# Opening with lengths taken without the rms and context pieces moved to the prologue; first cross attention with four copies in flight, far keys in 32 pieces and leading pairs copied

## The chip, the core and the metric

The kernel is one program on one core of a Trainium2 chip. The metric is device time in microseconds, lower is better. A core has TensorE (PE), VectorE (DVE), ScalarE (ACT), GpSimd (POOL) and SyncE (SP), which here issues nearly all transfers, and 16 DMA engines. The engines run their own instruction lists in order and wait for one another by semaphores that the kernel sets by hand.

## The reference

A decoder of two layers on `x` of 1024 tokens x 128 features, with 6404 context rows of 96 features. Each layer adds an attention-like block, a cross attention and a mixture of experts, each behind a layer norm. The change touches the first two blocks of layer 0:

```python
# block 1: fast weights (4 heads of 32, chunks of 256 tokens)
qkv = hidden @ qkv_w.T; q, k, v = split(qkv)
q, k = rms_norm(q, q_norm_w), rms_norm(k, k_norm_w)   # x * rsqrt(mean(x*x) + eps) * w, over 128 features
q, k = l2_normalize(heads(q)), l2_normalize(heads(k)) # x / (norm(x) + 1e-5), over 32 features
lr = softplus(hidden @ lr_proj_w.T + lr_proj_b + c)   # three rates per head and token
for each chunk:                                       # output with the weights W0, W1, W2 so far, then
    dw0, dw1, dw2 = gradients of the chunk with the rates; five Newton-Schulz rounds each
    W = (W + dw) renormalised to its first row lengths
# block 2: cross attention, 8 heads of 16, 1024 queries, 6404 keys
q, k, v = ln(x) @ Wq + bq, ctx @ Wk + bk, ctx @ Wv + bv
x = x + softmax(q k^T / 4) v @ Wo + bo
```

The second cross attention (layer 1) uses the same context with other weights (`wkv1`, 8 heads of 64, normalised keys).

## The kernel before

The program is a row of stages, each a block of five instruction lists: `opening_stage`, `xattn0_stage`, `moe0_stage` and three more. A stage starts on all engines when the one before has ended on all. The diff touches the first two.

**Opening.** It does two jobs at once. Job one is block 1: layer norm, the projections, rms norm, lengths and rates (the prologue), three updates of the fast weights (chunks 0 to 2), the outputs of the last chunk, and the queries of the first cross attention, which are split into three bf16 parts, stored to `q0_dram` and read back as `qs` and `qm` (the tail). Job two, the context, projects 52 tiles of 128 context rows to keys and values of both cross attentions and stores them in DRAM. `context()` on each engine is a generator; `Filler` takes pieces of it at named points of job one: `fill("ms")` takes as many pieces as the table `FILLS` says for "ms". Each engine uses the same table. A tick is four pieces, and there are 55 ticks for 52 tiles, since a tile passes through several ticks; so there are 220 pieces. The tables before give 37 pieces to the prologue (`FILLS`), 50 to each update and 26 to the tail (`FILLS_END`); the 7 left are run by `fill.rest()`. In a tick, PE computes `a_V` (L562, L563: keys and values of this stage's cross attention), `a_K` (L570) and `a_V` again (L574) and transposes (L581); ACT evacuates; DVE sums squares and scales; POOL splits the keys in four operations (L357 to L360) and raises sums to the power -1/2 (L365).

In the prologue DVE multiplies `qkv` with the rms factor (L814), then with the norm weight (L817); ACT squares it, DVE sums the squares to lengths (L833), ACT takes roots (L484), DVE divides (L840). POOL computes the rms factor (L374). `rated` (L846) multiplies keys or values with a rate, one instruction for each of 8 tiles, for three outputs.

The first context matmul waits for nine loads (`load_c`), the last being `null_v`. SP issues one broadcast of the byte mask `real` of 6656 columns to 96 partitions before the first context tiles.

In the tail SP waits for the first half of the split queries, stores it to `q0_dram` (L306), later reads it back and so lets the next stage begin.

**First cross attention.** The softmax needs a maximum for each query and head. Keys lie in SBUF as `ks` (and `ks0` for the first 2048 columns of the near heads, loaded in the opening). The near heads are 0 to 3 and the far heads 4 to 7. There are four units (head group x half of the queries); a unit has 104 pairs, each pair being two matmuls (L1192) of 128 queries by 496 keys for two heads, whose maxima are wanted, and 52 tiles of scores (L1210), exponentials (L1164) and weighting (L1223).

Unit 0's pairs come before any score. Of each four, three are matmuls into `psE`, copied as bf16 to `copied` by ACT (L1153) and merged into `running` by DVE (L1320); the fourth goes to one of three banks `psM` and is reduced by DVE (L1305). With `copied` of two slots, ACT waits for the merge of two pairs earlier:

```python
if n >= 2:
    e.wait_ge(pre_merged, n - 1)
```

Then DVE folds `running` (L1327, L1330), gives the maxima (L1338 to L1346), PE transposes them, ACT copies them to `mrow` (L1135), and SP writes them into rows of `qs` (L1107); the first scores wait for that (`m_placed`). Between, twelve pairs of unit 1 (`LEAD`) are computed and reduced. In each tile of units 0 to 2 two or three pairs of a later unit are computed and reduced between the scores (`in_tile`), so that the pairs of unit 2, the first that needs far keys, begin near tile 44 of unit 0.

SP issues near key block 1, the queries of units 1 to 3, near blocks 2 and 3, and all far keys in eight transfers of 832 KB; then, in each unit, the three rows of maxima and the value tiles, two tiles at a time, each when the tiles two turns back are used.

## Time and profile before

| | |
|---|---|
| median of 3 runs | 2792.28 us (2788.86 to 2794.58) |
| profiled execution, its own time | 2790.04 us |
| its span | 2788.3 us |
| PE busy | 2408.3 us (86%) |
| DVE busy | 2085.6 us (75%) |
| ACT busy | 1536.6 us (55%) |
| POOL busy | 297.7 us (11%) |

Times in the trace are microseconds from the span's start. The opening runs to 365.4 us, the first cross attention from there to about 1010 us, the other stages fill the rest. Busy time is the union of an engine's instructions in a stretch; the number in brackets behind it counts instructions. The PE clock is the granted share of full speed. In a timeline row the first number is the start, the second the length, in brackets stands the idle time of the engine just before and what ended it. SPq is the queue of SP's transfers.

### The profile page before, as it was taken

The numbers are of one execution on the slowest core, as the hardware profiler recorded it, in microseconds if no ns is written. First come the engines' busy times: TensorE is split into PE (matmuls) and PEld (weight loads), VectorE is DVE, ScalarE is ACT, GpSimd is POOL, SyncE is SP. The second block draws the span as 40 slices with busy tenths as digits, with TensorE's granted clock in tenths as the row PEclk, the third lists the DMA queues.
The fourth block names the chain that finished last, engine by engine and source line by source line (L and its number), as shares of the span: only waits on it lengthen the run. The fifth ranks groups of instructions, "written<-read, shape, count | busy, mean of one in ns | idle before, by whom it ended". The sixth has DMA issues, their size and how long they took to land. (4 is left out here: it accounts for less than half of the span.)

```text
span 2788.3 us, 34759 instructions
## 1 busy us (share of the span) xinstructions
PE 2408.3 (86%) x10287; PEld 892.3 (32%) x10344; DVE 2085.6 (75%) x3063; ACT 1536.6 (55%) x1850; POOL 297.7 (11%) x330
## 2 busy tenths in 40 slices
PE   5888755999999979999566579999999999997998
PEld 3555411222222224444223123333333333332443
DVE  5666678999997023344597789999999999977675
ACT  5544565776767953333343466666676766654111
POOL 4655600000000000000055000000000000000000
PEclk8988955999999989999688679999999999998998
DMA  4344498000000107766100522013113111111100
GB/s 116 129 137 136 136 154 93 25 25 25 25 23 27 31 26 190 192 192 181 25 0 5 124 65 58 27 42 92 29 30 89 43 29 29 29 35 36 80 1 8
DMA packets 186929, 190.79 MB, mean 68 GB/s; under 512 B 18496, under 2 KB 158981, under 8 KB 185473
## 3 DMA queue, kind: packets, MB, share of 16 engines
q1 hardware_dynamic: 186653, 188.97, 26.2%
q8 instruction: 78, 1.28, 0.2%
q14 instruction: 54, 0.44, 0.1%
q10 hardware_dynamic: 144, 0.10, 0.0%
HBM read 144.12 MB, written 41.42 MB: 67 GB/s over the span
## 5 line engine op out<-in xcount | busy, mean ns | idle before, releaser
L2520 DVE TENSOR_TENSOR y_acc<-y_acc,y_probs 128x1024 f32<-128x1024 f32 x408 | 496.5, 1217 | 34.0 <-ACT y_probs L2216 23.7
L2216 ACT ACTIVATE y_probs<-y_E,y_mask_bias 128x1024 f32<-128x1024 f32 x416 | 441.2, 1112 | 66.3 <-PE y_E L2301 47.1
L1164 ACT ACTIVATE x_probs<-x_E 128x1024 f32<-128x1024 f32 x408 | 396.8, 1021 | 137.0 <-PE x_E L1210 134.3
L1305 DVE TENSOR_REDUCE x_maxima<-x_M 128x1 f32<-128x496 f32 x676 | 420.5, 668 | 25.4 <-PE x_M L1192 14.0
L2310 PE MATMUL y_O<-y_probs,y_values 128*64 128x512 f32 x1664 | 402.3, 604 | 0.0
L2300 PE MATMUL y_E<-y_qa,y_ks 128*128 128x512 f16 x832 | 319.5, 384 | 1.2 <-ACT y_copied L2192 1.2
L2301 PE MATMUL y_E<-y_qb,y_ks 66*128 66x512 f16 x832 | 317.7, 382 | 0.0
L2192 ACT ACTIVATE y_copied<-y_M 128x1024 bf16<-128x1024 f32 x164 | 167.9, 1024 | 209.7 <-PE y_M L2267 209.7
L2458 DVE TENSOR_REDUCE y_maxima<-y_M 128x2 f32<-128x1024 f32 (+1 forms) x195 | 238.8, 1224 | 35.6 <-PE y_M L2267 23.4
L1629 DVE TENSOR_TENSOR f_hidden<-f_act_out,f_spread 128x512 f32<-128x512 f32 x160 | 110.7, 692 | 169.5 <-ACT f_act_out L1513 161.9
L1223 PE MATMUL x_O<-x_probs,x_values 128*32 128x512 f32 x1632 | 217.3, 605 | 0.9 <-ACT x_probs L1164 0.6
L1513 ACT ACTIVATE f_act_out<-f_b 128x512 f32<-128x512 f32 x160 | 95.4, 597 | 185.1 <-PE f_b L1545 185.1
L1210 PE MATMUL x_E<-qs,x_keys 128*128 128x512 bf16 x641 | 177.6, 382 | 8.9 <-issue 3.8
L2267 PE MATMUL y_M<-y_ks,y_qa 64*128 64x512 f16 x742 | 148.6, 397 | 26.4 <-DVE y_maxima L2458 23.7
L1550 PE MATMUL f_b<-f_hidden,f_weights 128*128 128x512 f32 x320 | 164.1, 596 | 5.0 <-DVE f_hidden L1629 5.0
L1545 PE MATMUL f_b<-f_xnT,f_weights 128*128 128x512 f32 x320 | 165.2, 598 | 1.1 <-ACT f_act_out L1513 1.1
L2310 PEld LDWEIGHTS y_O<-y_probs,y_values 128*64 128x64 f32 x1664 | 101.5, 136 | 171.2 <-issue 159.7
L2469 DVE TENSOR_TENSOR y_running<-y_running,y_copied 128x1024 bf16<-128x1024 bf16 x192 | 131.3, 684 | 3.7 <-ACT y_copied L2192 3.4
L1192 PE MATMUL x_M<-x_keys,qs 64*128 64x496 bf16 x298 | 117.0, 393 | 12.7 <-DVE x_maxima L1305 12.6
L2300 PEld LDWEIGHTS y_E<-y_qa,y_ks 128*128 128x128 f16 x832 | 81.6, 98 | 141.5 <-issue 45.5
L2713 PE MATMUL g_b<-g_w_in,g_xnT 128*128 128x512 f32 x256 | 117.7, 605 | 5.1 <-DVE g_gate L2783 3.9
L2267 PEld LDWEIGHTS y_M<-y_ks,y_qa 64*128 64x128 f16 x742 | 35.8, 93 | 259.7 <-DVE y_maxima L2458 174.4
(471 smaller groups left out, 3179.4 us busy)
## 6 DMA issues: line engine op xcount, KB each, us to landing
f_spread<-comb_dram SPq DMA_DIRECT2D x160, 256.0 KB, 3.9
y_values<-v_dram SPq DMA_DIRECT2D x208, 128.0 KB, 2.2
v_dram<-a_v_out SPq DMA_DIRECT2D x26, 512.0 KB, 2.7
k_dram<-a_k_parts SPq DMA_DIRECT2D x26, 512.0 KB, 3.4
x_values<-v_dram SPq DMA_DIRECT2D x100, 128.0 KB, 2.1
f_weights<-f_w_in SPq DMA_DIRECT2D x80, 128.0 KB, 2.3
y_ks<-k_dram SPq DMA_DIRECT2D x75, 128.0 KB, 2.9
v_dram<-a_v_out SPq DMA_DIRECT2D x26, 256.0 KB, 2.0
```

The lines of the kernel that those rows point to most:

```text
L1164: nc.scalar.activation(probs[:, n % 2, 2 * g:2 * g + 2, :], psE[:, 2 * g:2 * g + 2, :], ACT.Exp).then_inc(exped, 1)
L1210: ins = T.matmul(psE[:, j, :], key_tile(4 * (u // 2) + j, t), qs[:, u, j, :], start=True, stop=True)
L1223: ins = T.matmul(psO[32 * j:32 * j + 32, :], values[:, i, 32 * j:32 * j + 32], probs[:, n % 2, j, :], start=(t == 0), stop=(t == TILES0 - ...
L1305: V.tensor_reduce(maxima[:, 2 * h + j, qt, c:c + 1], psM[(2 * entry + j) % 3][:, 0:CHUNK0], AX.X, ALU.max).then_inc(max_done, 1)
L2192: A(out, scores, ACT.Copy).then_inc(S["spare_copied"], 1)
L2216: A(probs[:, i, :], psE[:, 2 * (i % 2):2 * (i % 2) + 2, :].rearrange("p a b -> p (a b)"), ACT.Exp, bias=mask_bias[:, bass.ds(c * TILES_IN_ ...
L2267: ins = T.matmul(out[:, j, :], qa[r, u, j, q0:q0 + P], ks1[r, u // 2 % 2, c * 512 + KVP * j:c * 512 + KVP * j + 512], start=True, stop=True)
L2300: T.matmul(psE[:, 2 * slot + j, :], ks1[:, u // 2 % 2, keys], qa[:, u, j, :], start=True, stop=False)
L2301: ins = T.matmul(psE[:, 2 * slot + j, :], ks2[:, u // 2 % 2, keys], qb[:, u, j, :], start=False, stop=True)
L2310: ins = T.matmul(psO[u % 2][DH1 * j:DH1 * j + DH1, :], values[:, i, DH1 * j:DH1 * j + DH1], probs[:, i, 512 * j:512 * j + 512], start=Fals ...
L2458: V.tensor_reduce(maxima[:, u % 2, :, 2 * g, bass.ds(c, 1)], psO_pair[:] if (u, g) == (0, 1) else psM[:], AX.X, ALU.max)\
L2520: ins = V.tensor_tensor(acc[:, u % 2, :], acc[:, u % 2, :], probs[:, i, :], ALU.add)
```

## The change

Opening: the tables move 17 context pieces from the tail and the rest to the prologue. The product with the norm weight comes first and alone; lengths are taken of it, and the rms factor enters through the 64 lengths (times rms, plus 1e-5, reciprocal, times rms). The `rated` products become one instruction each. The roots of the first weights are taken with those of the lengths, and small ACTIVATE instructions on `table` place table loads. `real` is broadcast in two parts, and `null_v` moves to the later list of loads.

First cross attention: `copied` gets four slots; eight of the twelve leading pairs are copied by ACT to `lead_max` and folded by DVE in four parts in unit 0's tiles 2, 4, 6 and 8; near blocks 2 and 3 are issued ahead of the queries; far keys are loaded in 4 blocks of 8 pieces, one behind each of the value loads 2 to 33.

```diff
-FILLS = (("stats", 4), ("xn", 2), ("proj0", 4), ("proj1", 4), ("sums", 4), ("ms", 4), ("qk", 4), ("hs", 3),
-         ("tr0", 4), ("tr1", 4))
+FILLS = (("stats", 4), ("xn", 3), ("proj0", 4), ("proj1", 4), ("sums", 6), ("ms", 8), ("qk", 6), ("hs", 6),
+         ("tr0", 6), ("tr1", 7))
-FILLS_END = (("last0", 4), ("last1", 4), ("q_stats", 4), ("q_norm", 4), ("q_tr", 5), ("q_split", 5))
+FILLS_END = (("last0", 2), ("last1", 2), ("q_stats", 3), ("q_norm", 3), ("q_tr", 3), ("q_split", 3))
-        LOADS_C, LOADS = 9, 10
+        LOADS_C, LOADS = 8, 11
-                sp.dma_start(real[0:CTX, :], d.real_keys.partition_broadcast(CTX)).then_inc(spread_real, 16)
+                sp.dma_start(real[0:CTX, INVERT_AT[0]], d.real_keys[INVERT_AT[0]].partition_broadcast(CTX))\
+                    .then_inc(spread_real, 16)
...
+                sp.dma_start(real[0:CTX, REST], d.real_keys[REST].partition_broadcast(CTX)).then_inc(spread_rest, 16)
-                e.wait_ge(to_sqrt, 1)
-                ACTIVATE(ninit[:], wn[:], ACT.Sqrt).then_inc(from_sqrt, 1)
...
+                e.wait_ge(s_qk, 1)
+                e.wait_ge(to_pow, 2)
+                ACTIVATE(sq[:], qk[:], ACT.Square).then_inc(s_sq, 1)
                 fill("ms")
...
-                e.wait_ge(s_qk, 1)
-                ACTIVATE(sq[:], qk[:], ACT.Square).then_inc(s_sq, 1)
                 fill("qk")
                 e.wait_ge(to_sqrt, 2)
-                ACTIVATE(hn[:], hs[:], ACT.Sqrt).then_inc(from_sqrt, 1)
+                ACTIVATE(ninit[:], wn[:], ACT.Sqrt)
+                ACTIVATE(hn[:], hs[:], ACT.Sqrt).then_inc(from_sqrt, 2)
+                ACTIVATE(table[:], half[:, 0:1], ACT.Sigmoid)
...
+                        if r == 2:
+                            ACTIVATE(table[:], half[:, 0:1], ACT.Sqrt)
...
                     ACTIVATE(wr[:], wn[:], ACT.Sqrt).then_inc(from_sqrt, 1)
+                    ACTIVATE(table[:], half[:, 0:1], ACT.Sigmoid)
...
+                V.tensor_tensor(qk[:].rearrange("p t a b -> p t (a b)"), qkv[:, :, 0:256],
+                                norm_w[:].unsqueeze(1).to_broadcast([P, TILES, 256]), ALU.mult).then_inc(s_qk, 1)
...
-                fill("ms")
-                e.wait_ge(from_pow, 2)
-                step(V.tensor_tensor(qk[:], qkv[:, :, 0:256].rearrange("p t (a b) -> p t a b", a=2),
-                                     rms[:].rearrange("p (t a) -> p t a", a=2).unsqueeze(3)
-                                     .to_broadcast([P, TILES, 2, P]), ALU.mult))
...
+                step(V.tensor_tensor(heads(hn), heads(hn), by_rms, ALU.mult))
                 step(V.tensor_scalar(hn[:], hn[:], 1e-5, None, ALU.add))
                 step(V.reciprocal(hs[:], hn[:]))
+                step(V.tensor_tensor(heads(hs), heads(hs), by_rms, ALU.mult))
+                fill("hs")
...
-        copied = sb("copied", [P, 2, 2, CHUNK0], BF16)
+        copied = sb("copied", [P, 4, 2, CHUNK0], BF16)
+        lead_max = sb("lead_max", [P, 8, 2, CHUNK0], BF16)
...
-                load_keys(near, KEY_BLOCKS[1], keys_in[1])
+                for b in (1, 2, 3):
+                    load_keys(near, KEY_BLOCKS[b], keys_in[b])
...
-                load_keys(far, slice(0, KVP), far_keys_in)
...
+                        if 2 <= g < 2 + 4 * (len(K_ROWS) + 1):
+                            load_far_piece(g - 2)
...
-                    if n >= 2:
-                        e.wait_ge(pre_merged, n - 1)
-                    nc.scalar.activation(copied[:, n % 2, :, :], psE[:, 2 * (n % 2):2 * (n % 2) + 2, 0:CHUNK0],
+                    if n >= 4:
+                        e.wait_ge(pre_merged, n - 3)
+                    nc.scalar.activation(copied[:, n % 4, :, :], psE[:, 2 * (n % 2):2 * (n % 2) + 2, 0:CHUNK0],
...
+                for i in range(COPIED_LEAD):
+                    n = 3 * EARLY + i
+                    e.wait_ge(pre_mm, 2 * n + 2)
+                    nc.scalar.activation(lead_max[:, i, :, :], psE[:, 2 * (n % 2):2 * (n % 2) + 2, 0:CHUNK0],
+                                         ACT.Copy).then_inc(pre_copied, 1)
...
+                def fold_lead(part):
+                    width = CHUNK0 >> part
+                    if part == 0:
+                        e.wait_ge(pre_copied, 3 * EARLY + COPIED_LEAD)
+                    if part < 3:
+                        step(V.tensor_tensor(lead_max[:, :, :, 0:width // 2], lead_max[:, :, :, 0:width // 2],
+                                             lead_max[:, :, :, width // 2:width], ALU.max))
+                    else:
+                        for h in range(2):
+                            ins = V.tensor_reduce(maxima[:, 2 * h:2 * h + 2, 0:4, 0].rearrange("p j q -> p q j"),
+                                                  lead_max[:, 4 * h:4 * h + 4, :, 0:width], AX.X, ALU.max)
+                        step(ins)
```

## Rows read from the trace of the kernel before

**Rows 1.** Busy time of each engine in stretches: instructions in brackets, PE clock, DMA share, GB/s.

```profile
78.70:157.90 79.20, 67.20 (x321) 44.60 (x320) 53.27 (x104) 40.92 (x95) 49.18 (x67) 0.94 0.43 138
...
365.40:458.80 93.40, 55.26 (x210) 10.91 (x210) 76.89 (x131) 72.66 (x78) 0.27 (x1) 0.50 1.03 130
...
481.00:893.00 412.00, 392.58 (x2365) 100.09 (x2412) 385.73 (x633) 293.75 (x306) 2.54 (x2) 1.00 0.09 24
```

**Rows 2.** Timeline of one turn of the maxima loop: start, length, engine, line, count.

```profile
442.73 0.68 DVE L1320 TENSOR_TENSOR x_probs<-x_probs,x_copied 128x992 bf16<-128x992 bf16 x1 [0.54 <-ACT x_copied L1153]
...
443.32 1.25 DVE L1305 TENSOR_REDUCE x_maxima<-x_M 128x1 f32<-128x496 f32 x2
...
444.48 1.25 DVE L1320 TENSOR_TENSOR x_probs<-x_probs,x_copied 128x992 bf16<-128x992 bf16 x2
...
445.24 2.80 ACT L1153 ACTIVATE x_copied<-x_E 128x992 bf16<-128x992 f32 x3 [0.75 <-PE x_E L1192]
446.27 0.68 DVE L1320 TENSOR_TENSOR x_probs<-x_probs,x_copied 128x992 bf16<-128x992 bf16 x1 [0.54 <-ACT x_copied L1153]
```

**Rows 3.** Timeline from the loop's end to the first scores of unit 0.

```profile
458.79 3.26 DVE L1327 TENSOR_TENSOR x_probs<-x_probs 128x2976 bf16<-128x2976 bf16 x3
...
464.57 0.19 DVE L1346 CAST x_mpf<-x_mpart 128x48 f32<-128x48 bf16 x1
...
466.03 0.27 ACT L1135 ACTIVATE x_mrow<-x_M 48x128 bf16<-48x128 f32 x1 [9.15 <-PE x_M L1230]
...
467.07 13.50 DVE L1305 TENSOR_REDUCE x_maxima<-x_M 128x1 f32<-128x496 f32 x20 [1.02 <-PE x_M L1192]
...
480.98 1.48 PE L1210 MATMUL x_E<-qs,ks 128*128 128x512 bf16 x3 [0.34 <-issue]
```

**Rows 4.** Single lines: lengths in ns (least, median, most), first and last start.

```profile
L1327 DVE TENSOR_TENSOR x_probs<-x_probs x3: 547/935/1708, 458.8 to 461.5; 128x2976 bf16<-128x2976 bf16 x1, 128x1488 bf16<-128x1488 bf16 x1, 128x744 bf16<-128x744 bf16 x1
...
L1330 DVE TENSOR_REDUCE x_maxima<-x_probs x2: 532/538/543, 462.1 to 462.5; 128x6 f32<-128x372 bf16 x2
...
L846 DVE TENSOR_TENSOR a_xn<-a_qk,a_lrate x8: 282/284/291, 66.9 to 68.3; 128x128 f32<-128x128 f32 x8
```

**Rows 5.** DMA issues in 367 to 371.4: KB each, median us to landing.

```profile
x_keys<-key_ones_in SPq DMA_DIRECT2D x1, 248.0 KB, 15.1
```

**Rows 6.** DMA issues in 100 to 250, the opening.

```profile
ks<-k_dram SPq DMA_DIRECT2D x7, 256.0 KB, 5.0
```

**Rows 7.** DMA issues in 480 to 1000, the units.

```profile
qs<-x_mrow SPq DMA_DIRECT2D x9, 4.0 KB, 1.8
```

**Rows 8.** Timeline of the prologue: the first context matmul and the rms products.

```profile
12.40 2.07 PE L570 MATMUL a_K<-a_wkv,a_ctx_real 97*128 97x512 f32 x2 [12.40 <-DMA a_null_v<-null_v_in]
...
45.55 2.29 DVE L814 TENSOR_TENSOR a_qk<-a_qkv,a_rms 128x2048 f32<-128x2048 f32 x1 [0.53 <-POOL a_rms L374]
45.59 2.53 POOL L357 TENSOR_TENSOR a_kr<-a_kf,a_k_parts 128x128 f32<-128x128 f32 x1
...
51.70 0.37 ACT L439 ACTIVATE a_kf<-a_V,a_bk 128x128 f32<-128x128 f32 x1 [7.60 <-POOL a_k_parts L360]
```

**Rows 9.** Timeline of the opening's tail: the queries' own chain.

```profile
323.39 0.41 DVE L867 TENSOR_TENSOR x<-x,a_b 128x256 f32<-128x256 f32 x1
...
327.20 1.64 DVE L56 BATCH_NORM_STATS2 a_stats<-x 128x6 f32<-128x128 f32 x8
...
329.87 1.65 POOL L374 TENSOR_TENSOR a_rstd<-a_var,a_mhalf 128x8 f32<-128x8 f32 x1 [1.22 <-DVE a_var L61]
...
333.87 2.80 DVE L67 TENSOR_SCALAR a_xn<-x,a_moments,a_rstd 128x128 f32<-128x128 f32 x8
...
338.74 0.60 ACT L537 ACTIVATE a_xnT<-a_b 128x512 f32<-128x512 f32 x1 [0.26 <-PE a_b L725]
...
342.53 1.88 PE L730 MATMUL a_b<-a_xnT,a_wq 128*128 128x512 f32 x4
...
355.69 0.68 SPq L306 DMA_DIRECT2D q_dram<-a_q_parts  x1
```

More of the change, by code:

```diff
@@ L1096, in _, with load_far_piece @@
                     sp.dma_start(dst, src).then_inc(load, 16)
-                for b in (2, 3):
-                    load_keys(near, KEY_BLOCKS[b], keys_in[b])
-                load_keys(far, slice(0, KVP), far_keys_in)
+                def load_far_piece(n):
+                    b, piece = n // (len(K_ROWS) + 1), n % (len(K_ROWS) + 1)
+                    cols, loaded = FAR_BLOCKS[b], far_keys_in[b]
+                    if piece < len(K_ROWS):
+                        load_key_rows(sp, d, ks[:, far, cols], far, cols, *K_ROWS[piece], loaded)
+                    else:
+                        load_key_ones(sp, d, ks[:, far, cols], cols, loaded)
                 for u in range(UNITS):
@@ L1375, in _ @@
                         merge(3 * (p // 4) + p % 4, p)
-                take(1, 0, EARLY)
-                pass_on(m_row, 1, EARLY + 1)
-                for p in range(1, LEAD):
-                    take(1, p, EARLY + 1 + p)
+                pass_on(m_row, 1, EARLY)
+                for p in range(COPIED_LEAD, LEAD):
+                    take(1, p, EARLY + 1 + p - COPIED_LEAD)
                 for u in range(UNITS):
```

72 lines of the change are left out of this document (40 added, 32 removed).

## Prediction

> **What bounds the kernel now.** I read the table by stage first, then the timelines of the stretches that the diff touches, then single lines and the transfers. The reader should see four stretches. The opening stage (0 to 365.4 us) keeps no engine full: in an update of 79.2 us PE is busy 67, DVE 53, POOL 49 [rows 1]. Its length is that of a chain of dependent small steps into which pieces of the second job, the keys and values ("context"), are threaded on every engine in a fixed order. The maxima before the first softmax tile (365.4 to 458.8) are a loop of 26 turns of four pairs. One turn is 3.54 us, from DVE's 442.73 to its 446.27; in it ACT makes three copies in 2.80 us and then stands, and DVE does five operations 0.59 us apart (2.93 us) and then waits 0.54 us for ACT [rows 2]. Each waits for the other, because the two copy buffers let ACT run only two pairs ahead, and DVE spends 1.17 us of each turn on the fourth pair, which it reduces straight from PSUM. Third comes the hand-over, 458.8 to 481: DVE folds alone, then reduces twelve leading pairs of the next unit at 1.36 us each, with PE waiting, before the first scores at 480.98 [rows 3]. Last come the units: in 481 to 893 DVE is busy 386 of 412 us and PE 393, so DVE work added there is paid [rows 1].
>
> **The loop with four copies in flight.** ACT may now be four pairs ahead. It needs three copies, 2.80 us less the overlap, near 2.7 us a turn; DVE needs 5 x 0.585 = 2.93 us. PE issues the fourth pair only when DVE has freed a bank, about half a microsecond before DVE's turn ends, which still leaves ACT its 2.7 us. I take 2.95 us a turn: 26 x (3.54 - 2.95) = 15.3 us saved. Bounds: 2.93 gives 15.9; if the order on PE (three copied pairs, then the one that waits for DVE) holds ACT up by half of its present wait, the turn is 3.3 and 6 us are saved; a loss is excluded, since no wait is added.
>
> The cover is the arrival of keys. The last piece of key block 1 is issued at 370.9 and lands 15.1 us later, at 386.0 [rows 5]; PE's first matmul of turn 8 needs it. PE runs one turn ahead of DVE, whose first operation is at 367.3: 367.3 + 7 x 2.95 = 388.0. Blocks 2 and 3 are now issued right behind it instead of behind 27 query transfers. Two MB took 16 us there, so block 2 (2 MB) is in near 402, wanted at 413; block 3 (0.7 MB) near 408, wanted at 436; the queries (1.5 MB) near 420, wanted at 441. Nothing is late, with 2 us to spare at the tightest place; a late block would cost its lateness once.
>
> **The leading pairs.** Eight of twelve go through ACT into a buffer of their own, 8 x 0.9 = 7.2 us, while DVE does its 6.0 us of folding and splitting of unit 0's maxima (458.79 to 464.76) [rows 3]. ACT starts some 2 us before DVE ends the loop, so it is free within the time in which DVE gives the maxima. The transpose of the maxima no longer waits for a leading pair's reduction, which saves 0.7 us. After the row of maxima is copied (466.03 + 0.27) the scores now start 14.7 us later [rows 3]. With four pairs left: 0.1 + 3 x 1.36 + 0.6, and the gap of 0.3 that stands before the scores now, 5.2 us. The row's own transfers must have landed too: three issues 1.9 us and 1.8 us to land when the queue is quiet [rows 7], 3.7 us, below 5.2. (Before, they landed behind the 6.8 MB of far keys.) Saved: 14.7 - 5.2 + 0.7 = 10.2 us. If the transfers still meet queries it is 8.
>
> **What it costs: the fold.** DVE halves 16 x 496 values three times and reduces the rest in unit 0's tiles 2, 4, 6 and 8. The halvings of the present fold took 1.708, 0.935 and 0.547 us for 2976, 1488 and 744 values [rows 4], that is 0.16 + 0.52 us a thousand. For 3968, 1984 and 992: 2.22 + 1.19 + 0.68 = 4.1 us; two reductions of 496 values by the 0.538 us for 372: 1.3 us. Sum 5.4 us. Of it DVE's idle share of unit time, 6% [rows 1], hides a little: 5 us on the path. Bounds 3 and 5.4 us. The banks just turn by two; the sequence of pairs is unchanged.
>
> **Far keys in 32 pieces.** They leave the start, where the DMA engines are full (share 1.03 [rows 1]), and follow value loads 2 to 33, one every two tiles (5.2 us). A piece is 213 KB. A piece of 256 KB of the same kind took 5.0 us to land in the opening [rows 6], so one of 213 is in before the next value load is issued. The value load goes out ahead of its piece. The first far chunk is wanted near tile 44 of unit 0, its eight pieces are issued by tile 18; the fourth block is issued by tile 14 of unit 1 and wanted near tile 32. I cost this at nothing; the cover is the 5.2 us of two tiles.
>
> First cross attention: -15.3 - 10.2 + 5.0 = -20.5 us (-22 to -10).
>
> **The opening.** The context job has 220 pieces (55 ticks of four). Before: 37 in the prologue, 150 in three updates, 26 in the tail and 7 left over. After: 54, 150, 16, 0. So 17 pieces move ahead of the updates, and since the last ticks only finish tiles, the tail keeps little but its own chain.
>
> Tail. Its delays can be read [rows 9]: the statistics start at 327.20 though the sum was done at 323.80 (3.4 us); the norm is applied at 333.87 though its power was done at 331.52 (2.3); the query matmul starts at 342.53 though its input was done at 339.34 (3.2). From there, first half out of PE (1.0), two copies (1.3) and four splitting steps (2.5) would allow the store to q_dram at 347.5; it is issued at 355.69 (8.2). Sum 17.1 us of context ahead of the chain. Sixteen pieces remain with about two ticks of real work, which cost some 2 us: -15 us. Bounds: -17 (all) and -11 (a third stays). The 9.7 us from that store to the next stage's start stay.
>
> Prologue. Seventeen pieces cost at least POOL's work per piece in an update, 49.2 / 50 = 0.98 us, and at most an update's pace, 79.2 / 50 = 1.58 us [rows 1]: 17 to 27 us. Against that: the first context matmul waits until 12.40 for null_v, the last of nine loads, behind a 639 KB broadcast [rows 8]; null_v leaves the list and the broadcast shrinks to 160 KB, about 2.4 us. The product of 2048 values with the rms (2.29 us) goes, replaced by two of 64 values; and lengths no longer wait for POOL's power. In the present trace that product and the next hold POOL's 0.43 us subtraction for 2.53 us and ACT waits 7.60 us for POOL [rows 8]: some 5 of these 7.6 go. The 24 rate products of 0.28 us [rows 4] become three of about 1.15 us (half of 2.29): 1.5 us, as part lies beside the transposes. The savings sum to 11 to 13 us. Net +4 to +16; I take +9, since ticks in the prologue ran slower than POOL's floor. What is late next is POOL, whose 54 pieces need 53 us at least in the 78 behind the first.
>
> The table switches only move: one Sqrt in the prologue falls away (1.28 us of ACT), the others stand where ACT had slack. I cost them at nothing (0 to 1.3 us gained).
>
> On the port: in [rows 8] POOL's subtraction took 2.53 us, and ended with DVE's 2048-value product. The Trainium skill (SBUF — State Buffer, section SBUF: two separate sides) says that a DVE operation with two SBUF inputs and a GpSimd one exclude each other for a whole instruction. That speaks against merging eight short products into one. By that rule POOL can be held up to 1.15 us three times, where it slipped between the short ones before; the sum would be 2 to 3 us worse in the prologue.
>
> Opening: +9 - 15 = -6 us (-14 to +4).
>
> **Sum.** -20.5 - 6 = -26.5 us against the profiled execution's own 2790.0: 2763.5. That execution lies 2.2 us under the median of the three runs, 2792.3, whose counterpart is 2765.8. Everything behind the first cross attention keeps its code; I expect 2765.
>
> **Rivals.**
> 1. The prologue takes the moved pieces at an update's pace with few savings (+15) and the tail keeps a third of its delay (-11): the opening gives +4, total -16.5, 2776. For it: the prologue's nine ticks take 66 us now, 12.4 to 78.7. Against: 7.6 us of one of them are the wait that goes. Chance 0.17.
> 2. The loop stays bound by the round of PE, ACT and bank release (3.3 us a turn): 10 us less, 2775. For it: PE's fourth pair waits for DVE, in order, in front of the next copied one. Against: five DVE operations fill 2.93 us, and only the copies were late. Chance 0.15.
> 3. The opening hides nearly all moved pieces (+2, -16): 8 us more, 2757. For it: DVE and ACT have a third idle. Chance 0.13.
> 4. Slower: far pieces hold up value loads. If a piece and the value load behind it took longer than the 5.2 us of two tiles, each excess would be paid 32 times; the gain of 26.5 us is gone from 0.83 us each. At 7 us per pair of transfers: 32 x 1.8 = 58 us, 2823. For it: 5.0 us to land for 256 KB. Against: most of these 5.0 us shared the DMA engines with the opening's stores, and loads overlap. Chance 0.04.
> 5. No change: fold, late keys and a full prologue together eat the gain, as if the four buffers bought nothing. Chance 0.02.
>
> **How the numbers follow.** The forecast as worked has 0.49; its own range is 2757 to 2771. The 8-in-10 range takes in rivals 1 and 2 up to 2779 and rival 3 down to 2751. A change under 0.2% (5.6 us) can't be told from none by such runs. Faster 0.94, same 0.02, slower 0.04.
>
> **What would show it.** A loop turn of 2.95 us with ACT never waiting for DVE; first scores some 90 us after the loop's first matmul instead of 115.4; four DVE operations on lead_max in tiles 2 to 8 with PE waiting there; no DMA share of 1.0 beyond the first 55 us of the stage; the first update's start near 88 instead of 78.7; from the last update's end (now 315.4) to the q_dram store 25 us instead of 40.3. Wrong would be: ACT waits that stay, value loads with a landing above 4 us, or a prologue beyond 95 us.

## The result, and the profile after

The changed kernel took 2743.65 us (median of 4 runs, 2743.25 to 2745.59), the kernel before 2791.59 (4 runs, 2788.86 to 2794.58): a ratio of 0.9829 with a 95% interval of 0.9812 to 0.9846. It is 48 us faster. The prediction, 2765 with a range from 2751 to 2779, is wrong: the direction holds, but the gain lies beyond the range. The profiled execution took 2743.25 us, its span is 2741.5.

Cutting both spans (2788.3 and 2741.5) at the same instructions shows where the 46.8 us come from. The updates are measured from the first Sigmoid of the first update to the last copy into `w1t_bd` of the third.

| stretch | before | after | change | forecast |
|---|---|---|---|---|
| start to the first update | 79.98 | 88.38 | +8.4 | +9 |
| three updates | 235.4 | 219.6 | -15.8 | 0 |
| tail, to the first matmul of the next stage | 50.2 | 33.2 | -16.9 | -15 |
| loop of the maxima | 93.2 | 77.8 | -15.4 | -15.3 |
| hand-over to the first scores | 22.2 | 11.85 | -10.35 | -10.2 |
| units, first scores to the first of the two sum matmuls that end them | 530.8 | 538.1 | +7.4 | +5 |
| everything behind | 1776.6 | 1772.5 | -4.1 | 0 |

Four of the five terms of the sum came out within 2 us; the updates were never in the sum. Their three lengths, cut at the starts of the same instructions and added up, show in which steps the time went. `gsum` is the sum of the squared gradient, `X` its normalised form, `wsq` the squared new weights, the root that of their row sums. e3, e5 and e12 are runs told below.

| step of the three updates, us | before | after | e3 | e5 | e12 |
|---|---|---|---|---|---|
| to `gsum` | 54.3 | 46.6 | 56.8 | 47.8 | 45.1 |
| `gsum` to `X` | 12.8 | 12.3 | 12.7 | 12.3 | 12.3 |
| `X` to `wsq`, with five rounds | 132.7 | 130.3 | 138.2 | 133.0 | 131.8 |
| `wsq` to the root | 13.9 | 9.9 | 11.9 | 13.2 | 13.2 |
| root to its use on DVE | 4.8 | 2.6 | 9.3 | 1.2 | 1.2 |
| use to the last copies | 16.9 | 17.9 | 16.9 | 18.8 | 19.0 |

Windows of the kernel after, with the columns of [rows 1]: the first update, the loop of the maxima, and the first 412 us of the units.

```profile
88.40:163.00 74.60, 63.91 (x313) 42.48 (x312) 52.48 (x103) 39.00 (x94) 47.65 (x67) 0.95 0.51 161
341.40:419.00 77.60, 58.14 (x216) 11.00 (x212) 74.71 (x130) 74.13 (x81) 0.00 (x0) 0.50 0.69 87
430.90:842.90 412.00, 388.54 (x2322) 98.74 (x2364) 384.80 (x625) 287.41 (x299) 2.52 (x2) 0.99 0.15 40
```

In the loop DVE is busy 74.7 of 77.6 us and ACT 74.1, where in [rows 1] they stood 16.5 and 21 us; the DMA share is 0.69 instead of 1.03. In the units DVE and PE are as busy as before, so what is added there is paid. The first update does the same work per engine within 4 us, and from its Sigmoid to that of the second are 74.6 us where there were 77.4 (79.98 to 157.37).

Timeline of one turn of the loop, which answers to [rows 2].

```profile
410.77 5.69 ACT L1171 ACTIVATE x_copied<-x_E 128x992 bf16<-128x992 f32 x6
...
411.89 1.25 DVE L1331 TENSOR_REDUCE x_maxima<-x_M 128x1 f32<-128x496 f32 x2
...
413.06 1.83 DVE L1346 TENSOR_TENSOR x_probs<-x_probs,x_copied 128x992 bf16<-128x992 bf16 x3
...
414.81 1.25 DVE L1331 TENSOR_REDUCE x_maxima<-x_M 128x1 f32<-128x496 f32 x2
```

From 411.89 to 414.81 is a turn of 2.92 us (forecast 2.95). No DVE row has a wait any more, and the six copies of ACT touch each other. The 0.54 us of waiting on ACT's copy is gone from DVE.

Timeline from the loop's end to the first scores, which answers to [rows 3].

```profile
416.60 7.22 ACT L1176 ACTIVATE x_lead_max<-x_E 128x992 bf16<-128x992 f32 x8
...
419.01 3.26 DVE L1353 TENSOR_TENSOR x_probs<-x_probs 128x2976 bf16<-128x2976 bf16 x3
...
425.48 0.27 ACT L1153 ACTIVATE x_mrow<-x_M 48x128 bf16<-48x128 f32 x1 [1.65 <-PE x_M L1253]
...
426.48 5.34 DVE L1331 TENSOR_REDUCE x_maxima<-x_M 128x1 f32<-128x496 f32 x8 [1.50 <-PE x_M L1215]
...
430.86 1.49 PE L1233 MATMUL x_E<-qs,ks 128*128 128x512 bf16 x3 [0.33 <-issue]
```

ACT copies the eight leading pairs (7.22 us) beside DVE's folding, as the sum had it. From the row of maxima (425.75) to the scores are 5.1 us, forecast 5.2.

Single lines of the fold, and the transfers of 480 to 970, which answer to [rows 4] and [rows 7].

```profile
L1365 DVE TENSOR_TENSOR x_lead_max<-x_lead_max x3: 666/1184/2215, 443.4 to 458.3; 128x3968 bf16<-128x3968 bf16 x1, 128x1984 bf16<-128x1984 bf16 x1, 128x992 bf16<-128x992 bf16 x1
L1369 DVE TENSOR_REDUCE x_maxima<-x_lead_max x2: 660/660/660, 463.9 to 464.5; 128x8 f32<-128x496 bf16 x2
```

```profile
x_values<-v_dram SPq DMA_DIRECT2D x91, 128.0 KB, 2.2
x_keys<-k_dram SPq DMA_DIRECT2D x21, 208.0 KB, 3.7
```

The halvings take 2.22, 1.18 and 0.67 us (forecast 2.22, 1.19, 0.68) and the two reductions 1.32 (forecast 1.3). A far piece lands in 3.7 us, inside the 5.2 of two tiles, and a value load in 2.2.

Timeline of the opening: the first context matmul, and the tail that answers to [rows 9].

```profile
9.34 2.05 PE L576 MATMUL a_K<-a_wkv,a_ctx_real 97*128 97x512 f32 x2 [9.34 <-DVE a_ctx_real L754]
```

```profile
313.29 0.42 DVE L873 TENSOR_TENSOR x<-x,a_b 128x256 f32<-128x256 f32 x1 [0.60 <-PE a_b L645]
...
314.95 1.63 DVE L56 BATCH_NORM_STATS2 a_stats<-x 128x6 f32<-128x128 f32 x8
...
330.78 0.54 SPq L308 DMA_DIRECT2D q_dram<-a_q_parts  x1
```

The statistics start 1.2 us after the sum instead of 3.4, and the store to `q_dram` comes 22.8 us after the last update instead of 40.3.

So the question is why three updates whose own code is nearly the same take 15.8 us less. Two things could have changed them: the pieces of context work beside each step, and the three small activations on `table`.

### The profile page after: what moved, and what is told of

The parts are those of the page before. It is cut to its first block and busy times, and to the rows that moved or that the text cites. A ratio compares the mean times of both kernels' runs of the same rounds, so it can differ in the third digit from the quotient of the medians.

```text
span 2741.5 us, 34784 instructions
## 1 busy us (share of the span) xinstructions
PE 2398.3 (87%) x10287; PEld 882.6 (32%) x10344; DVE 2072.4 (76%) x3032; ACT 1539.8 (56%) x1863; POOL 295.2 (11%) x330
## 3 DMA queue, kind: packets, MB, share of 16 engines
q8 instruction: 78, 1.28, 0.2%
## 5 line engine op out<-in xcount | busy, mean ns | idle before, releaser
L1331 DVE TENSOR_REDUCE x_maxima<-x_M 128x1 f32<-128x496 f32 x660 | 409.8, 667 | 28.0 <-PE x_M L1215 17.4
```

What stands on the lines that cost most here:

```text
L1331: V.tensor_reduce(maxima[:, 2 * h + j, qt, c:c + 1], psM[(2 * entry + j) % 3][:, 0:CHUNK0], AX.X, ALU.max).then_inc(max_done, 1)
```

## The experiments

Two names are used below. The *position* of an update is the number of a tick's four pieces that are already taken when it starts: 37 pieces ahead leave 1, and since an update takes 50, the next stands at 3, the third at 1. With 54 pieces ahead the positions are 2, 0, 2. *Tables* are the activations on `table`. Lengths of single updates run from the end of the one before (for the first, from its Sigmoid).

### The two stages apart, and the tables alone

The theory at this point was that order or amount of the moved pieces shortens the updates; the rival, that the table loads do.

**e1_opening_only** and **e2_xattn_only** take one stage from each kernel:

```diff
 # e1: the opening of after, and from here on the code of before
-        copied = sb("copied", [P, 4, 2, CHUNK0], BF16)
+        copied = sb("copied", [P, 2, 2, CHUNK0], BF16)
...
 # e2: the opening of before, and from here on the code of after
-FILLS = (("stats", 4), ("xn", 3), ("proj0", 4), ("proj1", 4), ("sums", 6), ("ms", 8), ("qk", 6), ("hs", 6),
-         ("tr0", 6), ("tr1", 7))
+FILLS = (("stats", 4), ("xn", 2), ("proj0", 4), ("proj1", 4), ("sums", 4), ("ms", 4), ("qk", 4), ("hs", 3),
+         ("tr0", 4), ("tr1", 4))
...
```

> The changed opening with the first cross attention of before. The trace of the changed kernel puts 24.3 us of the gain in the opening (first matmul of the next stage at 341.2 us instead of 365.6). If the two halves of the change are independent, this kernel gains 24 us and its next stage starts at 341.2 us; the loop of maxima keeps its 3.54 us a turn. If the far keys and the opening interact (shared DMA engines, the state of the PE clock), the sum of this kernel's and the other half's gains differs from the whole by more than 3 us.

> The opening of before with the changed first cross attention. By the changed kernel's trace its loop takes 2.92 us a turn and the stretch from the stage's first matmul to the first scores shrinks by 25.8 us, the units pay 7.4 us: net 18 us gained, stage to the end of unit 3 from 646.2 us to 627.8. If the halves are independent it is 18 us within 2 us; if the earlier start of the stage matters it is less.

e1 took 2763.51 us (ratio 0.991, 0.9894 to 0.9927), e2 2769.06 (0.9928, 0.9911 to 0.9945), the kernel before on that chip 2788.58. The gains are 25.1 and 19.5 us; their sum, 44.6, is 3 us short of the whole, which is what such medians scatter. The opening of e1 ends at 340.78, that of after at 341.22: the updates owe nothing to the next stage. In e2 the units took 535.9 us, 2.2 less than in the profile of after with the same code; that comes back below.

**e3_tables_only** is the kernel before with the small activations:

```diff
                 ACTIVATE(hn[:], hs[:], ACT.Sqrt).then_inc(from_sqrt, 1)
+                ACTIVATE(table[:], half[:, 0:1], ACT.Sigmoid)
...
                             query_gates(c, r)
+                        if r == 2:
+                            ACTIVATE(table[:], half[:, 0:1], ACT.Sqrt)
...
                     ACTIVATE(wr[:], wn[:], ACT.Sqrt).then_inc(from_sqrt, 1)
+                    ACTIVATE(table[:], half[:, 0:1], ACT.Sigmoid)
```

> The kernel before with only the small ACTIVATE instructions that place the table loads (Sigmoid after each root, Sqrt in round 2). Nothing else of the change. The updates went from 235.4 us to 219.6 us for all three. Theory T (table loads leave the path): the 1.28 us loads ahead of the first Sigmoid and ahead of the root were on the path, so the three updates lose 8 to 16 us here. Theory P (the position of the context's pieces against the update's chain, which 54 instead of 37 pieces shifts by one of four): nothing of the order of pieces changes here, so the updates keep 235 us within 4 us, which is what three loads of 1.28 us can give.

It took 2802.19 us, ratio 1.0043 (1.0026 to 1.006): slower by 13.6 us between the medians. The updates took 245.8 us instead of 235.4, and the first one starts 3.2 us later. As the sole cause, the tables fall. Both timelines stand at the end of the third update, before first, then e3: DVE waits for the context's squares, and ACT's queue shows why.

```profile
308.39 0.36 ACT L526 ACTIVATE a_wr<-a_wn 128x192 f32<-128x192 f32 x1
308.66 0.58 ACT L450 ACTIVATE a_ksq<-a_K 128x512 f32<-128x512 f32 x1
...
309.27 0.69 DVE L774 TENSOR_REDUCE a_ksum<-a_ksq 128x8 f32<-128x512 f32 x1 [0.94 <-ACT a_ksq L450]
309.88 0.25 DVE L937 TENSOR_SCALAR a_wr<-a_wr 128x192 f32<-128x192 f32 x1
```

```profile
320.48 0.36 ACT L529 ACTIVATE a_wr<-a_wn 128x192 f32<-128x192 f32 x1 [0.69 <-DVE a_wn L792]
320.86 1.28 ACT L530 ACT_TABLE_LOAD   x1
...
322.27 0.58 ACT L450 ACTIVATE a_ksq<-a_K 128x512 f32<-128x512 f32 x1
...
322.88 0.69 DVE L778 TENSOR_REDUCE a_ksum<-a_ksq 128x8 f32<-128x512 f32 x1 [1.83 <-ACT a_ksq L450]
323.48 0.25 DVE L941 TENSOR_SCALAR a_wr<-a_wr 128x192 f32<-128x192 f32 x1
```

The root `wr` is ready at 308.75 and at 320.84. What the chain does next on DVE (L937, L941 in e3) stands behind a context piece, and that piece needs ACT's squares, which now stand behind a load of 1.28 us. From the root's start to that of its use are 1.49 us before and 3.00 in e3. The load was placed "behind" the chain, but the chain waits through the context's piece. Over three updates this step costs 4.5 us (9.3 against 4.8). The Trainium skill (ScalarE: Activation LUTs, section What ACT_TABLE_LOAD costs) gives about 1283 ns for a load; the rows agree with 1.28 us.

The early Sqrt costs too: the third of the five rounds, where it stands, takes 10.2, 9.6 and 10.1 us instead of 9.1, 8.4 and 9.1, and in e6, below, the same within 0.2 us; the root comes 2.0 us sooner for it. Together that is 5.8 of the 10.4 us. The rest lies up to `gsum` (2.4) and in the other rounds, and has no cause that was shown.

### One piece

**e4_one_piece** is the kernel before with one piece more ahead of the updates and one less in the tail, no tables:

```diff
-         ("tr0", 4), ("tr1", 4))
+         ("tr0", 4), ("tr1", 5))
...
-... ("q_tr", 5), ("q_split", 5))
+... ("q_tr", 5), ("q_split", 4))
```

> The kernel before with one context piece moved from the last point of the tail to the last point of the prologue: 38 pieces ahead of the updates instead of 37, the rest as it was. Theory P: the three updates now meet the pieces in the positions 2, 0, 2 of a tick instead of 1, 3, 1, as in the changed kernel, and take 220 to 225 us instead of 235.4; the whole gains 10 to 15 us for one number in a table. Theory T: updates as before, the whole within 2 us.

It took 2776.68 us, ratio 0.9948 (0.9931 to 0.9965): one piece in 220 gives 12 us. The updates took 227.6 us instead of 235.4, and the tail 45.3 instead of 50.2. Why can be read at the first update. First DVE before, with one row of PE; then DVE in e4, with one row each of PE and ACT.

```profile
86.09 0.69 DVE L758 TENSOR_TENSOR a_k_parts<-a_T,a_k_parts 128x512 f16<-128x512 f32 x1 [2.34 <-ACT a_k_parts L430]
...
89.61 0.83 DVE L882 TENSOR_TENSOR a_dgb<-a_dgt,a_t 128x512 f32<-128x512 f32 x1
...
90.49 1.68 PE L656 MATMUL a_b<-a_dgb,a_xn 128*128 128x256 f32 x4 [3.76 <-DVE a_dgb L882]
...
96.12 0.36 DVE L891 TENSOR_TENSOR a_gsq<-a_grad 128x192 f32<-128x192 f32 x1 [2.72 <-ACT a_grad L510]
```

```profile
82.97 0.69 DVE L774 TENSOR_REDUCE a_ksum<-a_ksq 128x8 f32<-128x512 f32 x1 [1.84 <-ACT a_ksq L450]
...
89.45 0.83 DVE L882 TENSOR_TENSOR a_dgb<-a_dgt,a_t 128x512 f32<-128x512 f32 x1
90.33 1.13 PE L656 MATMUL a_b<-a_dgb,a_xn 128*128 128x256 f32 x4 [0.85 <-DVE a_dgb L882]
...
92.57 0.69 DVE L758 TENSOR_TENSOR a_k_parts<-a_T,a_k_parts 128x512 f16<-128x512 f32 x1 [1.19 <-ACT a_k_parts L430]
93.09 0.88 ACT L510 ACTIVATE a_grad<-a_b 32x64 f32<-32x64 f32 x4
...
94.39 0.49 DVE L891 TENSOR_TENSOR a_gsq<-a_grad 128x192 f32<-128x192 f32 x1
```

The Sigmoid of this update starts at 79.98 before and at 81.36 in e4. At position 1 the fill "hid" holds DVE for 2.34 us on a copy of transposes that PE made just before; PE then has nothing left and waits 3.76 us for `dgb`; and ACT's copies of the gradient stand behind a context piece, so DVE waits 2.72 us more. At position 2 other and shorter waits stand in their place: DVE waits 1.84 and 1.19 us, PE 0.85 us for `dgb`, and the copies of the gradient are done when DVE wants them. `gsum` starts 16.5 us after the Sigmoid before and 13.5 in e4. The same work is done; only the neighbours changed. TensorE's clock is not the cause: its mean over the three updates was 0.91 before and 0.88 in the shorter updates of e4.

### Pieces and tables in the kernel after

**e5_no_tables** takes the three activations out of after; **e6_53_pieces** moves one piece from its prologue to its tail; **e8_56_pieces** moves two the other way:

```diff
 # e5
-                ACTIVATE(table[:], half[:, 0:1], ACT.Sigmoid)
...
-                        if r == 2:
-                            ACTIVATE(table[:], half[:, 0:1], ACT.Sqrt)
...
-                    ACTIVATE(table[:], half[:, 0:1], ACT.Sigmoid)
...
 # e6
-         ("tr0", 6), ("tr1", 7))
-FILLS_END = (("last0", 2), ...
+         ("tr0", 6), ("tr1", 6))
+FILLS_END = (("last0", 3), ...
...
 # e8
-         ("tr0", 6), ("tr1", 7))
-... ("q_split", 3))
+         ("tr0", 7), ("tr1", 8))
+... ("q_split", 1))
```

> The kernel after without the three small activations on `table`; the pieces and everything else as after. Where the table loads fall changes how the updates run, and the earlier runs give three theories. Pieces alone: the updates are shorter because the 54 pieces ahead of them put other pieces beside each step of the chain, and tables add nothing: updates 220 us, total 2743 to 2745. Tables always cost what they cost when added alone to before (10.4 us of updates, 3.3 of prologue): updates 209, total near 2730. Both together: in the order with 38 pieces ahead and no tables the updates took 227.6 us, with 54 pieces and tables 219.6, so tables pay only where the pieces leave ScalarE free at the end of an update, and without them the updates take 227 to 228 and the total is near 2751. I expect the third.

> The kernel after with one piece moved from the prologue to the tail: 53 pieces ahead of the updates, 17 in the tail. If what counts is the amount of work moved, the change is one piece in seventeen: under 1.5 us, total 2743 to 2746. If what counts is which of a tick's four pieces stands beside which step of the update (53 gives the order of before, 54 the order of after), the updates go back to at least before's 235.4 us, and with the table loads, which added 10.4 us in that order, to about 245: total 2759 to 2770. I expect 2765.

> The kernel after with two more pieces ahead of the updates (56) and two less in the tail. By the order of pieces the updates then begin at the first, third and first piece of a tick instead of third, first, third. In the kernel after an update took 73.4 and 74.5 us where it began at the third and 71.7 at the first: 2 x 71.7 + 74 = 217.4, 2 us less; two pieces more in the prologue cost 1 to 2 us and give up to 1 in the tail. If order decides: 2741 to 2744. If only the amount moved counts: the same within 1 us. If two more pieces were enough to put the prologue on the path at an update's pace: 2746. These are close together; the lengths of single updates tell, the total may not.

e5 took 2750.39 us (0.9855, 0.9839 to 0.9872), e6 2768.43 (0.9926, 0.9909 to 0.9943), e8 2743.69 (0.9835, 0.9819 to 0.9851), with 2790.34 for the kernel before. The updates in us (those of e9, e10 and e12 follow):

| run | ahead, positions | tables | three updates |
|---|---|---|---|
| before, e2 | 37: 1, 3, 1 | no | 235.4, 234.9 |
| e3 | 37: 1, 3, 1 | yes | 245.8 |
| e6 | 53: 1, 3, 1 | yes | 245.1 |
| e4 | 38: 2, 0, 2 | no | 227.6 |
| e5 | 54: 2, 0, 2 | no | 226.3 |
| after, e1, e7, e11 | 54: 2, 0, 2 | yes | 219.6, 218.2, 219.1, 219.6 |
| e8 | 56: 0, 2, 0 | yes | 215.2 |

Sixteen pieces more or less (e3 and e6, e4 and e5) change nothing beyond 1.3 us; one piece changes 25.5 us (e6 and after). At odd positions the tables cost 10 us, at even ones they give 7. The gain of 15.8 us is order (235.4 to 226.3, 9.1 us) and, only in that order, tables (226.3 to 219.6, 6.7 us). By steps (the table further up), order alone gives its 9.1 us mainly up to `gsum` (6.5) and from the root to its use (3.6), and loses 1.9 on the last copies. In e5 the first Sigmoid also came late, at 91.15 against 88.4 to 89.9 in after, e1, e7, e11 and e12. e8 adds that an update at position 0 is shorter (69.1 and 70.2 us, 70.2 to 71.7 in after, e1, e7 and e11) than one at 2 (75.9, and 73.4 to 75.4); its 4.4 us were given back by the prologue, where the first Sigmoid moved from 88.38 to 93.93, so the total stood still.

Why position 0 is shorter shows in two steps. From `gsum` to `X` it takes 2.6 us, position 2 takes 4.8 or 4.9. And the first round takes 8.2 us at position 0, with TensorE's granted clock full in all such updates; at position 2 it takes 9.5 to 10.8 us with a mean clock of 0.75 to 0.87, in every run. The first rounds of the first two updates of after, at positions 2 and 0:

```profile
110.60:121.22 10.62, 10.62 (x47) 7.38 (x48) 6.47 (x13) 4.15 (x10) 3.72 (x6) 0.77 0.18 53
185.68:193.85 8.17, 8.17 (x47) 5.84 (x48) 5.54 (x11) 4.14 (x12) 4.08 (x7) 1.00 0.54 164
```

The end of the third update in the kernel after, where the load costs 0.1 us:

```profile
301.26 0.67 DVE L782 TENSOR_REDUCE a_ksum<-a_ksq 128x8 f32<-128x512 f32 x1
301.38 0.36 ACT L531 ACTIVATE a_wr<-a_wn 128x192 f32<-128x192 f32 x1 [0.35 <-DVE a_wn L796]
301.76 1.28 ACT L532 ACT_TABLE_LOAD   x1
301.86 0.24 DVE L943 TENSOR_SCALAR a_wr<-a_wr 128x192 f32<-128x192 f32 x1
302.13 1.35 DVE L944 RECIPROCAL a_wn<-a_wr 128x192 f32<-128x192 f32 x1
```

The context's reduction comes before the root here, so DVE goes on 0.48 us after the root's start, and the load lies beside the reciprocal. Without the activations (e5) the use follows 0.4 us behind the root. In the second update of after, at position 0, it follows after 1.35 us.

**e12_no_early_sqrt** takes only the early Sqrt out of after:

```diff
-                        if r == 2:
-                            ACTIVATE(table[:], half[:, 0:1], ACT.Sqrt)
```

> The kernel after without the small Sqrt activation in the third round of each update; the small Sigmoid ones stay. Without all three kinds the updates took 226.3 us against 218.2 to 219.6 in four runs with them. From the product wsq to the root of the row sums those four took 3.0 to 3.5 us in each update and the run without tables 4.4. If the early Sqrt only takes its load of 1.28 us out of that step: 3 x 1.1 = 3.3 us more, updates 222 to 223, total 2746 to 2748. If it carries the whole gain of the tables: 226, total 2750. If the gain is that of the Sigmoid placed behind the root, which takes its load from the start of the next update: 219 to 220, total 2743 to 2745. I expect the first.

It took 2747.45 us (0.985, 0.9834 to 0.9867; before 2788.73), the updates 222.6, as the first of the three theories has it. The step from `wsq` to the root is 4.4 us in each update against 3.4, 3.0 and 3.4 in after, 3.3 us in all; the use then comes 1.4 us sooner behind the root and the last copies 1.1 us later behind it, so the whole way from `wsq` to the last copies is 3.0 us longer, as the updates are. So the early Sqrt is worth 3 of the 6.7 us that the tables give in this order. The rest would belong to the Sigmoid loads: e5, without them, is 3.7 us longer than e12, and 2.7 of these lie between an update's start and its `gsum`. Whether the load itself is on the path there is not shown; at the third update of e5 it ends at 241.63, 1.06 us before the Sigmoid, which waits for PE.

### Every update at position 0

**e9_48_each** and **e10_52_each** give each update a multiple of four pieces, starting from 56 and 52:

```diff
 # e9
-         ("tr0", 6), ("tr1", 7))
-FILLS_UPDATE = (("wtot", 3), ("root", 2), ("wT", 3))
-FILLS_END = (("last0", 2), ("last1", 2), ("q_stats", 3), ("q_norm", 3), ...
+         ("tr0", 7), ("tr1", 8))
+FILLS_UPDATE = (("wtot", 3), ("root", 2), ("wT", 1))
+FILLS_END = (("last0", 3), ("last1", 3), ("q_stats", 4), ("q_norm", 4), ...
...
 # e10
-         ("tr0", 6), ("tr1", 7))
-FILLS_UPDATE = (("wtot", 3), ("root", 2), ("wT", 3))
-... ("q_stats", 3), ("q_norm", 3), ("q_tr", 3), ("q_split", 3))
+         ("tr0", 5), ("tr1", 6))
+FILLS_UPDATE = (("wtot", 3), ("root", 2), ("wT", 5))
+... ("q_stats", 2), ("q_norm", 2), ("q_tr", 2), ("q_split", 2))
```

> The kernel after with 56 pieces ahead of the updates, 48 instead of 50 in each update (the fill before the last copies of an update takes one piece instead of three) and 20 in the tail. Every update then begins at the first piece of a tick. If the order of pieces decides, each update takes what the first and third took with 56 pieces ahead (69.1 and 70.2 us) less up to 1 us for two pieces fewer: 204 to 208 us in all against 215.2 there; the prologue stays at 93.9; the tail, with four pieces more than after, takes 35 to 37 instead of 33.2: total 2734 to 2740. If the second update of that run was long (75.9) for another reason, for one its place among the transfers, one update stays near 75: total 2741 or more.

> The kernel after with 52 pieces ahead of the updates, 52 in each (five pieces before the last copies of an update) and 12 in the tail. Every update begins at the first piece of a tick. By the order of pieces each takes 69 to 70 us, and the two pieces more, which stand straight in front of the copies that end the update, cost 0.7 to 1.5 us each time: 211 to 215 us in all; the prologue ends 1 to 3 us earlier than with 54 (first Sigmoid 86 to 88.4), the tail keeps 33: total 2735 to 2741. By the amount of work alone the updates grow to 3 x 73.2 x 52 / 50 = 228: total near 2750.

e9 took 2740.28 us (0.9823, 0.9805 to 0.984), e10 2740.80 (0.9821, 0.9805 to 0.9838), before 2791.01. The updates took 210.0 and 217.0 us, each 2 us above its expected range: in e9 the second and third spend 1.8 us more up to `gsum` than in e10; in e10 the two pieces in front of the last copies cost 1.3 to 1.5 us each. That the amount of work alone sets an update (228 us for e10) is refuted. Both medians lie 3 us under the kernel after, but the intervals of the ratios overlap almost wholly (0.9812 to 0.9846 there): a gain over after is not shown.

### The fold and the clock

**e7_no_fold** leaves the fold out, **e11_split_fold** halves its first instruction:

```diff
 # e7
-                        if u == 0 and t in FOLD_AT:
-                            fold_lead(FOLD_AT.index(t))
...
 # e11
-        FOLD_AT = (2, 4, 6, 8)
+        FOLD_AT = (2, 3, 4, 6, 8)
...
-                    width = CHUNK0 >> part
-                    if part == 0:
-                        e.wait_ge(pre_copied, 3 * EARLY + COPIED_LEAD)
+                    if part < 2:
+                        if part == 0:
+                            e.wait_ge(pre_copied, 3 * EARLY + COPIED_LEAD)
+                        some = slice(4 * part, 4 * part + 4)
+                        step(V.tensor_tensor(lead_max[:, some, :, 0:CHUNK0 // 2], lead_max[:, some, :, 0:CHUNK0 // 2],
+                                             lead_max[:, some, :, CHUNK0 // 2:CHUNK0], ALU.max))
+                        return
+                    part -= 1
+                    width = CHUNK0 >> part
```

> The kernel after without fold_lead: the maxima of the eight leading pairs of unit 1 are left out. First scores to the sum of unit 3's maxima took 530.8 us before and 538.7 after. If the 7.9 us are VectorE's fold (2.2 + 1.2 + 0.7 + 1.3 us), some 5.4 come back: units 533, total 2738. If the fold also holds up TensorE beyond its own length, all 7.9 come back: 531, total 2736. If they are TensorE's granted clock, which stays at half for the first 5 us of the units after (it was full within 3 us before), under 2 us come back. I expect 5 to 6 us less, 2738.

> The kernel after with the first halving of lead_max (one instruction of 3968 values, 2.21 us) as two of 1984 values, in tiles 2 and 3. In the profiled run of after TensorE stood 1.9 us behind that instruction, its granted clock then fell to half for 4 us, and the units took 538.7 us; in four other runs with the same code it stood as long, the clock stayed full and the units took 535.5 to 535.9. Without the fold they took 532.6. If TensorE's pause is what the fold costs: each halving of 1.2 us then leaves a pause of under 0.9, units 534 to 535, total 2739 to 2742. If the cost is VectorE's busy time, which is the same in one or two instructions: 535.5 to 536. In both no second fall of the clock.

e7 took 2742.26 us (0.9833, 0.9816 to 0.9849), e11 2744.23 (0.9828, 0.9812 to 0.9844). In total times neither differs from after; e7's expected 2738 was missed. In the profiles the units took 532.1 us in e7 and 536.4 in e11. (The two expectations have 538.7 us for after and 532.6 for e7, taken to the second of the last two sum matmuls; to the first, as all others, it is 538.1 and 532.1.) Windows of 5 us in the first 20 us of the units in after, then in e8, whose code there is the same (the second of each is left out; its clock is 0.95 and 1.00); the third number from the end is the granted clock.

```profile
430.86:435.86 5.00, 4.74 (x13) 0.86 (x16) 1.70 (x4) 3.88 (x4) 0.00 (x0) 0.50 0.02 3
...
440.86:445.86 5.00, 3.50 (x25) 0.82 (x24) 4.88 (x7) 3.24 (x4) 0.00 (x0) 1.00 0.23 59
445.86:450.86 5.00, 4.43 (x18) 0.92 (x18) 3.55 (x6) 1.94 (x2) 0.00 (x0) 0.66 0.26 65
```

```profile
433.65:438.65 5.00, 4.74 (x19) 0.91 (x18) 1.94 (x4) 3.88 (x4) 0.00 (x0) 0.65 0.01 3
...
443.65:448.65 5.00, 2.93 (x22) 0.77 (x20) 4.91 (x6) 2.34 (x3) 0.00 (x0) 1.00 0.24 58
448.65:453.65 5.00, 4.93 (x32) 1.21 (x30) 4.93 (x8) 3.71 (x4) 0.00 (x0) 1.00 0.06 15
```

In both PE then stands 1.91 us behind the first halving. This is after; e8 has the same wait at 448.32 and then scores of 1.04 us instead of 1.89.

```profile
446.43 0.44 PE L1215 MATMUL x_M<-ks,qs 64*128 64x496 bf16 x1 [1.91 <-DVE x_maxima L1331]
...
446.80 1.89 PE L1233 MATMUL x_E<-qs,ks 128*128 128x512 bf16 x4
```

In after the clock falls to half behind the pause (0.66 over 5 us), and so it does in e10 and e12; there the units took 537.9 to 538.2 us. In e2, e5, e6, e8 and e9 it stays full, and they took 535.5 to 535.9. In e11 each pause is 0.9 us and the clock stays full behind them: 536.4. These runs also differ in the clock of the first 5 us, so those are to be compared in which it is equal. The first and the fourth 5 us of e11 (the first of e7 also has 0.50):

```profile
430.88:435.88 5.00, 4.74 (x13) 0.87 (x16) 1.70 (x4) 3.88 (x4) 0.00 (x0) 0.50 0.01 3
...
445.88:450.88 5.00, 4.11 (x26) 1.06 (x28) 4.97 (x8) 3.02 (x4) 0.00 (x0) 1.00 0.21 53
```

With 0.50 in the first 5 us in all three, after took 538.1, e11 536.4 and e7 532.1. So of the 7.4 us, 1.7 are the second fall of the clock (after less e11) and 4.4 the fold (e11 less e7). The same 4.4 come out where the fold is whole and the clock stays full behind it: e2 less e4 (0.59 and 0.56 in the first 5 us) is 535.9 less 531.5, e5 less e1 (0.68 and 0.66) 535.6 less 531.1. So the fold is paid as DVE's time whether in one piece or two, and these runs show no cost of PE's pause beyond it. The 1.3 us left go with the clock of the first 5 us, 0.50 against 0.75 before: e3, whose units have the code of before, took 531.9 us with 0.50.

## Why the prediction was wrong

**The step that failed** is in the part on the opening, which set the opening's 220 pieces out as "37 in the prologue, 150 in three updates, 26 in the tail" against "54, 150, 16", and costed prologue and tail alone. That the updates keep 150 pieces was read as: they keep their length. And of the activations it says "The table switches only move ... I cost them at nothing (0 to 1.3 us gained)". The runs put 15.8 us there: 9.1 for the order, 6.7 for the tables in that order. The numbers to see it stood in the prediction's own text: 37 and 54 leave remainders of 1 and 2 in ticks of four. With this term the sum would have been 42 us. None of the rivals was this mechanism, and the range did not reach it. The steps are 7.7 us up to `gsum`, 0.6 from there to `X`, 2.4 in the rounds and 6.2 from `wsq` to the use of the root, less 1.0 on the last copies.

**The opening's other terms.** Prologue +9: measured +8.4, with the first context matmul at 9.34 instead of 12.40 (3.1 us where 2.4 were taken). Tail -15: -16.9, at the bound "all". e4 adds a doubt on its reason: there the tail fell by 4.9 us for one piece, so part of the tail's delay was order too, and not the number of pieces.

**The merged products.** The forecast put a hold of POOL beside each merged product at 1.15 us, and did not count it in the sum. Timeline of after, POOL's power and copy beside the products of DVE:

```profile
69.92 2.40 DVE L848 TENSOR_TENSOR a_qk<-a_qk,a_hs 128x2048 f32<-128x2048 f32 x1
72.35 1.36 DVE L853 TENSOR_TENSOR a_xn<-a_qk,a_lrate 128x1024 f32<-128x1024 f32 x1
```

```profile
70.25 2.38 POOL L362 TENSOR_TENSOR a_k_parts<-a_kf,a_zeros 128x128 bf16<-128x128 f32 x1
72.71 2.51 POOL L367 TENSOR_TENSOR a_kroot<-a_ksum,a_mhalf 128x8 f32<-128x8 f32 x1
```

POOL's copy takes 2.38 us beside the 2048-value product and 0.51 one tick later (76.84), and its power 2.51 beside the first `rated` and 1.65 one tick later (77.43): 1.9 and 0.9 us held. The Trainium skill (SBUF — State Buffer, section SBUF: two separate sides) says that such a pair excludes each other for a whole instruction, and these rows agree. The `rated` product took 1.36 to 1.48 us, not 1.15. What of it lies on the path was not tried alone.

**The first cross attention.** Loop -15.3: -15.4. Hand-over -10.2: -10.35. Far pieces at nothing: right, 3.7 us to land. Fold +5: its 5.4 us of DVE were right to 0.1, and it cost 4.4, since idle time hid 1.0 us of it where 0.4 were taken. The units came to +7.4 in the profile of after, since the clock at half in the first 5 us added 1.3 and its second fall 1.7; the sum had no term for the clock. That e2, e5, e6, e8 and e9 came to +4.7 to +5.2, the forecast's number, is in part luck: fold and clock together made it.

**Slips in the working.** The bounds of the two halves do not follow from their parts: -22 to -10 for the first cross attention would be -23 to -9, and -14 to +4 for the opening -13 to +5. The terms of the hand-over (0.1 + 3 x 1.36 + 0.6 + 0.3) make 5.1 us, not 5.2; 5.1 were measured. None of this moves the forecast by more than 0.1 us.

**Behind the first cross attention** the code is the same, and from 1771.6 to 1776.8 us were measured there in the profiles of the fourteen kernels, with 1776.6 before and 1772.5 after. The 4.1 us are within that spread and have no cause that was shown. Together: updates -15.8, tail -1.9, prologue -0.6, fold and clock +2.4, rest -4.1, the two small ones -0.25, make the 20.3 us by which the spans' gain of 46.8 exceeds the forecast's 26.5.

## What to carry to other kernels

Where a second job is threaded into a chain by a fixed order on every engine, a count of pieces says what work is moved, and its remainder by the period of the job says who stands beside whom from there on: move a single piece, and read every wait of the chain again. A filler hides on an engine only if what it waits for does not itself stand behind the chain; a table load, or any other small thing put "off the path", is on it as soon as a filler's input is behind it and the chain's next step behind the filler. Cost a moved part on the stages that it passes over, not only on those that it leaves and enters.

## What the runs showed of the hardware

The same pause of TensorE, 1.91 us at the same place in the program, let the granted clock fall to half for 3.4 us in three profiled executions (after, e10, e12) and not in five others (e2, e5, e6, e8, e9); it is worth 1.4 to 1.8 us each time (537.9 to 538.2 us in the units against 536.4 in e11). In all three the clock had also been at half through the first 5 us of the units (0.50, against 0.59 to 0.70 in the five). That the two go together is observed, not explained.

In the updates the clock fell to half at the same place in every run with updates at even positions: the first round has a mean of 0.75 to 0.87 at position 2 and 1.00 at position 0, 9.5 to 10.8 us against 8.2. So the place of the filler also went with the clock at which the chain ran on.
